# Delta-rule attention with routed experts on one core: the output product in fp16 pairs, ten weight units' low parts on GpSimd, a half-width product, and a new order

## The reference

```
xn = layernorm(x)
q, k, v = xn@Wq, xn@Wk, xn@Wv        (4 heads, dk 128, dv 64);  beta = sigmoid(xn@Wb)
k = k / |k| ;  q = q * dk**-0.5
S_t = S_{t-1} + k_t (beta_t (v_t - k_t^T S_{t-1}))^T ;  o_t = q_t^T S_t
o = rmsnorm(o) * norm_w * silu(xn@Wg) ;  s = o @ Wo
e = argmax_e(xn @ router_w) per token;  f = relu(xn @ fc[e])**2 @ proj[e]^T
out = x + s * silu(f)
```

## Time and profile before

| | |
|---|---|
| median of 3 runs | 768.43 us (763.4 to 768.46) |
| the profiled execution | 766.95 us, its span 764.9 us |
| mean granted clock of TensorE | 0.959 |
| busy: PE, DVE, ACT, POOL | 689.6, 503.8, 489.2, 430.1 us |
| moved by DMA | 149.98 MB |

### The profile page before, as it was taken

The page is one execution under the profiler, slowest core; times in us unless marked ns, Lnnn a source line. Parts: engine busy times, 40 slices in busy tenths (PEclk is TensorE's granted clock), DMA queues, the critical chain, the costliest instruction groups (busy, mean ns, idle before and its releaser), DMA issues.

```text
span 764.9 us, 24691 instructions
## 1 busy us (share of the span) xinstructions
PE 689.6 (90%) x10090; PEld 592.3 (77%) x10090; DVE 503.8 (66%) x1053; ACT 489.2 (64%) x997; POOL 430.1 (56%) x434
## 2 busy tenths in 40 slices
PE   4775596788799999999999999999999999999984
PEld 3665475676598889888888888888888897888862
DVE  6779643554376764666666566777768676667784
ACT  5774245644476765686777777767776677668641
POOL 4750241446143752868686858585848567647624
PEclk9897599999999999999999999999999999999997
DMA  9777958866697766545545445333343443333085
GB/s 297 241 227 233 366 182 322 275 223 194 247 318 260 266 229 246 219 149 173 198 149 188 182 151 218 119 133 126 126 141 145 163 158 146 125 120 120 30 266 175
DMA packets 51071, 149.98 MB, mean 196 GB/s; under 512 B 4688, under 2 KB 25424, under 8 KB 40976
## 3 DMA queue, kind: packets, MB, share of 16 engines
q1 hardware_dynamic: 33904, 104.62, 37.5%
q10 hardware_dynamic: 13312, 33.56, 13.3%
q0 software_dynamic: 3744, 10.23, 4.4%
HBM read 118.11 MB, written 30.28 MB: 194 GB/s over the span
## 4 chain that ended last, share of the span: by engine, by line
PE 63%; DVE 4%; POOL 4%; DMA 3%; issue 3%; ACT 2%; POOLq 1%; DVEq 0%; ACTq 0%
PE bank L566 7%; PE bank L517 7%; PE bank L519 6%; PE bank L518 6%; PE bank L648 4%; PE bank L614 4%; PE bank L598 4%; PE bank L789 4%; PE bank L579 4%; PE bank L547 3%; PE bank L705 3%; PE bank L687 3%; PE bank L696 2%; DMA w_d<-x_first 2%; PE bank L627 2%
## 5 line engine op out<-in xcount | busy, mean ns | idle before, releaser
L2424 DVE TENSOR_TENSOR Pm<-bank,lvl_mask 128x256 f16<-128x256 f32 x180 | 68.2, 417 | 61.0 <-PE bank L687 59.4
L1487 ACT CAST Z<-bank 128x256 f16<-128x256 f32 x180 | 60.9, 376 | 56.0 <-PE bank L705 53.1
L566 PE MATMUL bank<-wts,h 128*128 128x256 f16 x648 | 92.3, 273 | 0.0
L2435 DVE TENSOR_TENSOR M<-bank,M 128x256 f16<-128x256 f32 x180 | 68.3, 417 | 33.7 <-PE bank L696 33.3
L3189 POOL TENSOR_TENSOR h<-hT,h 128x512 f16<-128x512 f32 x54 | 62.6, 1160 | 36.1 <-ACT hT L1432 35.8
L517 PE MATMUL bank<-xsT,wts 128*128 128x128 f16 x432 | 77.2, 219 | 0.0
L519 PE MATMUL bank<-xsT,wts 128*128 128x128 f16 x432 | 77.1, 219 | 0.0
L518 PE MATMUL bank<-xsT,wts 128*128 128x128 f16 x432 | 77.1, 219 | 0.0
L3222 POOL TENSOR_TENSOR XTl<-unit,XTh 128x512 f16<-128x512 f32 x32 | 39.8, 1244 | 52.1 <-ACT XTh L1504 52.0
L3180 POOL DMA_INDIRECT xs<-xn_d,from_row x39 | 42.1, 1080 | 42.6 <-DVE to_row L2334 35.6
L1422 ACT ACTIVATE hT<-bank 128x512 f32<-128x512 f32 x78 | 47.1, 605 | 24.9 <-PE bank L547 11.5
(11 more groups left out here) (268 smaller groups left out, 2413.5 us busy)
## 6 DMA issues: line engine op xcount, KB each, us to landing
wts<-w_d SPq DMA_DIRECT2D x54, 1024.0 KB, 6.8
w_d<-x_first ACTq DMA_DIRECT2D x32, 512.0 KB, 4.7
wts<-in_fc SPq DMA_DIRECT2D x12, 1024.0 KB, 6.9
wts<-in_pj SPq DMA_DIRECT2D x12, 1024.0 KB, 9.8
x_first<-in_fc ACTq DMA_DIRECT2D x16, 512.0 KB, 4.6
x_first<-in_pj ACTq DMA_DIRECT2D x16, 512.0 KB, 5.2
wts<-in_x SPq DMA_DIRECT2D x10, 512.0 KB, 7.8
wts<-y_d SPq DMA_DIRECT2D x4, 1024.0 KB, 10.2
```

What stands on the lines that cost most here:

```text
L566: ins = pe.matmul(psum[bank[0]][:, 0:D], h16[:, zh, c, :], pjw16[r][:, zw, c, :], start=(n == 0), stop=(n == 3 * HC - 1))
L2424: dve.tensor_tensor(h4(Pms[last(m)], b).rearrange("p h (n c) -> p h n c", c=s), half4(level_bank(m, b)).rearrange("p h (n c) -> p h n c", ...
L2435: dve.tensor_tensor(evens(h4(Ms[last(m)], b), s), half4(level_bank(m, b)).rearrange("p h (n c) -> p h n c", c=s), evens(h4(Ms[last(m)], b) ...
```

## The change

Five things are changed.

- The product with Wo uses fp16 pairs. Wo is loaded into the space of hT, weighted by norm_w and scaled by 64 there, and split once (weigh_wo, wo_low). Per chunk ogTc on ScalarE writes the high part of og's transpose, the new ogT_low on VectorE the low part; wo waits for both. s_cp takes the factor 64 out. The first relu of the experts waits until Wo is split.
- M's product with the identity, M0, is made for even columns only; M0c copies these, and MZ on VectorE writes the odd ones from the identity.
- The low parts of units 0 to 9 are made by GpSimd. Since it has only a subtraction here, ScalarE first scales the unit in place, in a pass of its own.
- Waits and counts follow from that.
- The lists of all engines are written in another order, in ramp, steps and tail.

```diff
+ON_POOL = 10
-        wo_sb = sb("wo_sb", [P, KC, D])
+        wo16 = sb("wo16", [P, 2, KC, D], F16)
-        ogT = sb("ogT", [P, B, KC, P])
+        ogT16 = sb("ogT16", [P, 2, B, KC, P], F16)
+        wo_raw = hT[:, 0:4, :].rearrange("p c n -> p (c n)")
...
@@ M0 (TensorE), M0c (ScalarE), MZ (VectorE)
-    ins = pe.matmul(bank4(level_bank(m, b))[:, h, :], Zs[last(m)][:, H * b + h, :], ident16[:],
+    ins = pe.matmul(half4(level_bank(m, b))[:, h, :], Zs[last(m)][:, H * b + h, :],
+                    evens(ident16[:].unsqueeze(1), 1)[:, 0].rearrange("p n c -> p (n c)"),
-    act.copy(h4(Ms[last(m)], b), bank4(level_bank(m, b))).then_inc(M0_ok[b], 1)
+    act.copy(evens(h4(Ms[last(m)], b), 1), half4(level_bank(m, b)).unsqueeze(3)).then_inc(M0_ok[b], 1)
+    dve.tensor_copy(evens(h4(Ms[last(m)], b), 1, 1), evens(ident16[:].unsqueeze(1).to_broadcast([P, H, P]), 1, 1))
...
@@ wo (TensorE)
-        pe.wait_ge(wo_ok, KC)
+        pe.wait_ge(wol_ok, WOL_FROM + 1)
     ch.on(ogT_ok)
+    pe.wait_ge(ogl_ok, c + 1)
-            ins = pe.matmul(psum[CH_BANK][:, b * D:(b + 1) * D], ogT[:, b, k, :], wo_sb[:, k, :],
-                            start=(k == 0), stop=(k == KC - 1))
+            ins = pairs(psum[CH_BANK][:, b * D:(b + 1) * D], [ogT16[:, z, b, k, :] for z in range(2)],
+                        [wo16[:, z, k, :] for z in range(2)], start=(k == 0), stop=(k == KC - 1))
...
@@ VectorE
+    def wo_low():
+        dve.wait_ge(wo_ok, 2)
+        dve.scalar_tensor_tensor(out=wo16[:, 1].rearrange("p k n -> p (k n)"), in0=wo_raw, scalar=W_SCALE,
+                                 in1=wo16[:, 0].rearrange("p k n -> p (k n)"), op0=ALU.mult,
+                                 op1=ALU.subtract).then_inc(wol_ok, 1)
+    def ogT_low(c):
+        At(dve, c).on(ogT_ok)
+        dve.tensor_tensor(ogT16[:, 1].rearrange("p b k n -> p (b k n)"), psum[CH_BANK][:],
+                          ogT16[:, 0].rearrange("p b k n -> p (b k n)"), ALU.subtract).then_inc(ogl_ok, 1)
...
@@ unit_high (ScalarE), unit_low (GpSimd, units 0 to 9)
+    if u < ON_POOL:
+        act.activation(unit_in[u % 2], unit_in[u % 2], ACT.Copy, scale=W_SCALE).then_inc(unit_hi, 1)
+        act.wait_ge(unit_hi, 2 * u + 1)
-    act.activation(unit_out[u % 2][:, 0], unit_in[u % 2], ACT.Copy, scale=W_SCALE).then_inc(unit_hi, 1)
+    act.activation(unit_out[u % 2][:, 0], unit_in[u % 2], ACT.Copy,
+                   scale=1.0 if u < ON_POOL else W_SCALE).then_inc(unit_hi, 1)
+    def unit_low(u):
+        pool.wait_ge(unit_hi, 2 * (u + 1))
+        pool.tensor_tensor(unit_out[u % 2][:, 1], unit_in[u % 2], unit_out[u % 2][:, 0], ALU.subtract).then_inc(unit_lo, 1)
...
@@ the orders, of step3 on TensorE the end
                     Dm(i, 5)
+                    experts(1)
                     wo(i - 1)
                     T(i, 5)
-                    experts(2)
+                    experts(1)
                     F(i)
```

More of the change, by code:

```diff
@@ L1692, in ramp @@
-                    y_sigmoid(0)
-                    X_h(1, 1)
-                    y_sigmoid(1)
+                    ksq_(2, 0)
+                    dZf_(0, 0)
+                    unit_load(14)
+                    dZf_(0, 1)
                     relu(2, 1)
                     P_h(1, 1)
+                    unit_load(15)
                     sq(2, 1)
+                    unit_store(12)
+                    X_h(1, 1)
                     U_h(0)
+                    sig(1, 1)
+                    unit_store(13)
@@ L1755, in ramp @@
-                    dZ(1, 2, 0)
+                    unit_store(19)
+                    dZ(1, 3, 1)
+                    keep_y(4)
+                    keep_rows(5)
+                    P_h(2, 1)
+                    unit_high(20)
+                    X_h(2, 0)
+                    dZ(1, 4, 0)
+                    s_cp(0)
+                    dZ(1, 4, 1)
+                    X_h(2, 1)
+                    relu(5, 0)
+                    relu(5, 1)
+                    sig(2, 0)
+                    unit_load(22)
@@ new lines, in ramp @@
+                    unit_high(26)
+                    relu(8, 1)
+                    s_cp(1)
+                    dZ(2, 5, 0)
+                    dZ(2, 5, 1)
+                    y_sigmoid(7)
+                    X_h(3, 1)
+                    unit_store(26)
+                    sq(8, 1)
+                    unit_load(27)
+                    unit_load(28)
+                    X_h(3, 0)
+                    R_h(2)
+                    keep_rows(9)
+                    dZf_(2, 0)
+                    dZf_(2, 1)
@@ L1842, in ramp @@
+                    U_h(2)
+                    unit_high(27)
+                    unit_high(28)
+                    unit_store(27)
+                    P_h(3, 0)
+                    unit_load(29)
+                    keep_y(8)
+                    osq(2)
+                    M0c(3, 0)
+                    sig(3, 1)
+                    M0c(3, 1)
                     P_h(3, 1)
-                    s_cp(1)
+                    relu(9, 0)
+                    ksq_(4, 0)
+                    sq(9, 0)
@@ new lines, in tail @@
+                    P_h(14, 1)
+                    U_h(13)
+                    relu(36, 0)
+                    X_h(14, 0)
+                    h_high(36, 0)
+                    relu(36, 1)
+                    ksq_(15, 1)
+                    sq(36, 0)
+                    osq(13)
+                    h_high(36, 1)
+                    sq(36, 1)
+                    q_h(15, 0)
+                    M0c(14, 0)
+                    M0c(14, 1)
+                    P_h(14, 0)
+                    keep_rows(37)
@@ L2652, in ramp @@
-                    Pm_(1, 2, 0)
+                    q_l(2, 1)
+                    X32(2, 1)
+                    S_l(0)
+                    ogT_low(0)
+                    Pm_(1, 4, 1)
+                    X32(2, 0)
+                    Pm_(1, 4, 0)
+                    P32(2, 1)
+                    dM(1, 4, 1)
+                    P32(2, 0)
+                    dM(1, 4, 0)
+                    unit_low(20)
+                    Pm_(1, 5, 1)
+                    R32(1)
+                    Pm_(1, 5, 0)
@@ new lines, in ramp @@
+                    og_(1)
+                    Pm_(2, 0, 0)
+                    Pm_(2, 0, 1)
+                    oss_(1)
+                    dM(2, 0, 1)
+                    dM(2, 0, 0)
+                    f_t(3, 0)
+                    f_t(3, 1)
+                    Pm_(2, 1, 0)
+                    Pm_(2, 1, 1)
+                    dM(2, 1, 0)
+                    dM(2, 1, 1)
+                    q_l(3, 0)
+                    S32_(1)
+                    Pm_(2, 2, 0)
+                    Pm_(2, 2, 1)
@@ L2880, in step2 @@
                     dM(i, 2, 1)
-                    S_l(i - 1)
+                    ogT_low(i - 1)
                     Pm_(i, 3, 0)
@@ L2910, in tail @@
                     MZ(13, 1)
+                    kss_(14, 1)
                     Zo(13, 1)
```

2052 lines of the change are left out of this document (990 added, 1062 removed).

## The result

The changed kernel takes **773.0 us** (median of four runs, 772.6 to 775.4); the kernel before took 767.3 us (763.4 to 768.5) beside it. The ratio is 1.009, with a 95% interval of 1.0046 to 1.0134. The forecast was 756, its range 746 to 768: the change was to make the kernel faster, and the time lies outside the range. The profiled execution has a span of 771.2 us, where that of before had 764.9.

What follows compares the result with a forecast made beforehand. TensorE bounds the stream, waits the ramp, one chain the end; 6.4 (stream) + 1.4 + 0 (ramp) + 0 + 3.5 (end) = 11.3 us off the profiled 766.95 gives 755.7, forecast 756 us, range 746 to 768.

Steps and rivals of the forecast that it cites:

- The stream: Nine steps where TensorE's own work is the time: 0.50 + 0.21 = 0.71 us saved per step, 6.4 us.
- The new order can add or take some tenths per step: Stream: waits of 0.2 to 0.3 us can show between TensorE's pieces; taken as 0, -2 to +4 us.
- I cost it at nothing there: Stream: VectorE's added work, about 1.6 us per step, priced at nothing because VectorE idles a third of the time.
- The cover of ogT_low: Steps: six or more TensorE pieces before wo hide this VectorE subtraction; uncovered, each step would lose 0.7 to 0.9 us.
- M's product: Product with the identity on TensorE, 0.45 us down to 0.24: 0.21 us saved per chunk, 3.4 us in all.
- The ramp: Before the stream: 1.4 us saved on TensorE after 200 us; the ten units' move 0, between 5 gained and 17.6 lost.
- The lock in the ramp: GpSimd subtractions blocking VectorE on the way to the gather: four overlaps cost 2.2 us, at worst 8.5.
- The end: Last chain: 3.1 us from less VectorE work behind og_(15), plus a faster last output product; together 3.5 us saved.
- A: Ramp shorter by more: gather 5 us earlier, stalls behind it shrink 3 to 5 us; 748 or 746 us; chance 0.20.
- B: Ramp slower: the units' detour through ScalarE and GpSimd costs up to 17.6 us, giving 773; chance 0.09.
- C: Half the gain eaten: VectorE held 8.5 us before the gather, or step hand-overs 6.3 us; 764 or 762; 0.24 with D.
- D: fp16 output product not faster, as it loads 12 sets of weights against 8; 762 us; chance 0.24 together with C.

Runs made afterwards that it cites:

- experiment 4: Kernel before in all its old orders, with fp16 output product and half-width M's product, no unit on GpSimd: 771.5 us, ratio 1.002.
- experiment 1: Changed kernel with send_y (indirect DMAs of expert outputs) and root_ moved last in GpSimd's stream-step lists: 758.7 us, ratio to before 0.988.
- experiment 6: Kernel before, old orders, with only M's product at half width and VectorE's copy of odd columns into M: 771.1 us.
- experiment 5: Kernel before, old orders, with the fp16 output product alone, M's product at full width: 771.7 us.
- experiments 11 and 12: 11: new ramp and tail, old step orders, fp16 output product, half-width M0 except two-tile steps, 753.6 us; 12: experiment 1 with full-width M0, 760.2 us.
- Experiments 8 and 9: 8: kernel before with only the ten units' low parts on GpSimd, 780.9 us; 9: experiment 1 with those units back on VectorE, 769.5 us.
- experiment 2: Changed kernel, new orders kept, with M's product at full width again and VectorE's copy into M gone: 773.3 us.
- experiment 3: Changed kernel with steps and tail in the old orders; all changed arithmetic and the new ramp kept: 761.0 us.

## Why the prediction was wrong, point by point

- **The stream, 6.4 us saved, "the firmest term": wrong, +19.0 us.** Two steps of the argument failed.
  - **"The new order can add or take some tenths per step ... I take 0, with -2 to +4 us for nine steps."** This is the step that decided. The new lists cost 356.3 - 337.2 = 19.1 us in nine steps (changed kernel against experiment 4), and experiment 1 gives back 15.2 of them with a change of GpSimd's list alone. In a held three-tile step 3.1 us are idle time of TensorE and 1.0 longer work at the lower clock behind it, a cost that the prediction did not have either. The prediction looked through TensorE's list for hand-overs; it did not lay GpSimd's new list beside VectorE's at the step boundary. There, before, three indirect DMAs ran beside the copies in a three-tile step; now one subtraction stands between the last two indirect DMAs and three behind them. In a two-tile step one subtraction stood beside the first copy before, too (1.06 us, under experiment 6). The lock itself was in the prediction, with the earlier trace rows, and so was the rule; both were applied to the ramp only.
  - **"I cost it at nothing there; it lies in the shadow of the wait for X_h and of the expert groups ahead of M0."** The copy into M stands on VectorE's path from U's products to Z's odd columns, not in a shadow, and in the two-tile steps of the old orders TensorE has nothing left to cover it with. It costs 0.6 us in a two-tile step against 0.21 saved (experiment 6). A mark was there: the copy of Z has a mean of 0.455 us. Its line in the kernel before, with minimum, median and maximum, says that it was being held in some steps already:

```profile
L2408 DVE COPY Z<-ident x30: 301/314/1076, 55.4 to 686.3; 128x256 f16<-128x256 f16 x30
```

- **The output product, 0.50 us a step: right.** Two-tile steps fell by 0.5 us (experiment 5). In three-tile steps 0.2 was left.
- **The cover of ogT_low: right**, by the same run.
- **M's product, 0.21 us a step on TensorE: right as work, of no worth as time.** 0.2 to 0.3 us is gained in three-tile steps of the old orders, 0.6 lost in two-tile ones; experiments 11 and 12 find no net gain. With both parts the nine steps save 0.1 us (experiment 4), not 6.4.
- **The ramp, 1.4 us plus 0 for the units: the sum was too low, and the mechanism missed.** It gained 8.4 us. The first gather is at 88.7 us, 2.4 later than before and just outside the 85 to 88 of the forecast; from it to R_l(3) pass 209.4 us instead of 220.1. Experiments 8 and 9 show an interaction: alone, the units cost about 13 us, and the new order without them about 11 against experiment 1. Adding parts one at a time can't find that. Which wait behind the gather became shorter is open. The ramp's sum also has no term for the preparation of the output product, which seems to cost some 8 us in the old order (experiment 5); in the new one it was not tried by itself.
- **The lock in the ramp, 2.2 us by its row, 8.5 at worst**: seen as one unit_low of 3.70 us instead of 2.12; its share in the ramp's sum was not isolated.
- **The end, 3.5 us saved: right in mechanism, too small.** From og_(15) to the end of the span pass 771.2 - 759.1 = 12.1 us, forecast 15, before 18.5. ogm(15) fell to 1.13 us, and the last product took 1.2 us, not 2.6, since the granted clock was 1.00 there and the forecast had taken the 0.50 of before. The tail as a whole gained 4.4, against 3.5: between R_l(12) and R_l(13) the new order lost 1.4 of it.
- **The rivals.** A (ramp shorter by more) has the size of the ramp's gain and not its way: the gather came 2.4 us later, not 5 earlier. B gave the right number, 773, by luck and by the wrong place: the detour costs only in the old order. C named the right lock and the wrong place; its step half, 6.3 us for nine steps, was a third of what came. D was wrong. The chances have a slip too: they give B's upper end to times above 776.1, while B in full is 773.

In one sum: the forecast took 11.3 us off the 767; measured were -8.4 (ramp), -4.4 (tail), -0.1 (new arithmetic in the steps) and +19.1 (new lists in the steps).

## What to carry to other kernels

Where VectorE and GpSimd both run instructions with SBUF operands, as here, a new order is priced by laying the two lists beside each other at the place that TensorE waits for, not by counting each engine's work. A short instruction whose mean is well above its median (here 0.455 against 0.314 us) may already be held in places, and what is added ahead of it on the same path is exposed. Read a mixed change by a marker once per step, and try its parts in the orders of before: here three good parts and one bad order together read as a small loss.

## What the runs showed of the hardware that was not expected

**A VectorE instruction can be held by several GpSimd instructions in a row.** The 4.18 us copy above outlasted three subtractions, and got no turn when the first or second of them ended. So did the product of two SBUF inputs in experiment 2, from 342.32 to 346.43 us, over the same three. In a two-tile step R_l got a turn after one. The timeline of VectorE, then of GpSimd, in the changed kernel:

```profile
546.15 2.49 DVE L2474 TENSOR_TENSOR R_l<-ru,R_h 128x512 f16<-128x512 f32 x1 [0.68 <-ACT R_h L1532]
```

```profile
545.80 1.09 POOL L3235 DMA_INDIRECT y_d<-y_sb,to_row  x1 [0.18 <-issue]
546.92 1.16 POOL L3264 TENSOR_TENSOR PTl<-f_t,PTh 128x512 f16<-128x512 f32 x1
548.03 1.19 POOL L3231 TENSOR_TENSOR y_sb<-y_sb,y_sg 128x256 f32<-128x256 f32 x1
```

GpSimd's PTl ended at 548.08, R_l at 548.64, and the GpSimd instruction behind PTl took 1.19 us, against 0.73 elsewhere. So a VectorE instruction is starved in one place and takes its turn in another, and the two are not told apart by copy or subtraction; what decides was not found. The Trainium skill, "SBUF — State Buffer", section "Who interferes with whom", says that a VectorE copy in a two-port mode, and a VectorE instruction with two SBUF inputs beside a GpSimd one that reads SBUF, contend with GpSimd, and that the one issued later waits for the whole of the other's instruction. This trace agrees in kind, for both sorts, and adds that the wait can last over three of them.

**What stands behind an indirect DMA on GpSimd matters to the VectorE copy beside it, and so does how far the DMA has run.** Both held copies began while an indirect DMA ran (342.26 within 341.70 to 342.67, 344.49 within 344.03 to 345.08) and should have ended before the subtraction behind it started; they did not. In experiment 1 a copy at 345.30, within an indirect DMA from 344.50 to 345.72 with another one behind it, took 0.31 us. In the changed kernel's two-tile steps the same kind of DMA has a subtraction of 128x512 behind it (549.50 to 550.52): the copy that began 0.19 us into it, at 549.69, took 0.31 us, the next, 0.40 us into it, took 2.00. And with GpSimd's small root_ (128x8) behind the DMA, a copy 0.45 us into it took 0.33 us (experiment 3, at 501.81). That a large subtraction waiting in line takes the port early would explain these; it was not tried by itself.
